# Attention with exponentials over blocks of three half steps, and the loop over batches written out

## The reference

```python
q = (xin @ wq.T + bq).reshape(b, s, H, DK)
k = (xin @ wk.T + bk).reshape(b, s, H, DK)
v = (xin @ wv.T + bv).reshape(b, s, H, DK)
scores = jnp.einsum('bshd,bthd->bhst', q, k) * (1.0 / np.sqrt(DK))
a = jax.nn.softmax(scores, axis=-1)
o = jnp.einsum('bhst,bthd->bshd', a, v).reshape(b, s, DH)
...
x1 = layernorm(xh + mha(xh, ...), g1, be1)
x2 = layernorm(xsh + mha(xsh, ...), g2, be2)    # xsh: the smoothed input
y = jnp.concatenate([x1, x2], axis=-1)
y_ff = relu(y @ w_ff1.T + b_ff1) @ w_ff2.T + b_ff2
out = x + layernorm(y + y_ff) + ffn(xn)
```

## Time and profile before

| what | us |
|---|---|
| median of 3 runs | 2676.5 (2676.16 to 2676.57) |
| the profiled execution | 2678.51 |
| its span, first to last instruction | 2677.0 |
| attention of one batch, first exponential to last | 492 to 498 |
| ACT, exponentials of attention, all | 1915.7 busy |
| PE, values (L1183) | 1071.4 busy |
| PE, scores (L1157) | 624.5 busy |

### The profile page before, as it was taken

How to read it: one execution, slowest core, us unless ns; L and a number is a source line. 1 busy time by engine, 2 the same in 40 slices (tenths; PEclk the granted TensorE clock), 3 DMA queues, 4 the chain that set the end, 5 groups by cost and what they waited for, 6 DMA issues and landing times.

```text
span 2677.0 us, 75084 instructions
## 1 busy us (share of the span) xinstructions
PE 2529.1 (94%) x30049; PEld 1004.4 (38%) x30049; DVE 1516.9 (57%) x3228; ACT 2190.8 (82%) x2411; POOL 355.2 (13%) x349
## 2 busy tenths in 40 slices
PE   5799999999999999998999999999999999999976
PEld 3233333335633333333663333333464333333344
DVE  5344555565764555556575455555567545555576
ACT  3699999994479999997449999999556999999933
POOL 0201010003410100000440101000144010100142
PEclk9899999999999999999999999999999999999988
DMA  4602010003120202000411102000041010100001
GB/s 159 122 10 34 10 34 10 10 10 104 50 65 10 34 14 38 10 6 12 115 49 57 30 14 34 10 10 6 21 122 48 10 34 10 34 10 10 6 25 45
DMA packets 50612, 96.38 MB, mean 36 GB/s; under 512 B 8768, under 2 KB 33344, under 8 KB 49872
## 3 DMA queue, kind: packets, MB, share of 16 engines
q1 hardware_dynamic: 41808, 71.99, 8.9%
q0 software_dynamic: 8448, 19.41, 4.4%
HBM read 57.23 MB, written 34.08 MB: 34 GB/s over the span
## 4 chain that ended last, share of the span: by engine, by line
PE 80%; DVE 7%; issue 5%; POOL 4%; ACT 1%; DMA 1%; SPq 0%; DVEq 0%; POOLq 0%; ACTq 0%
PE slot L1183 34%; PE slot L1157 20%; PE slot L994 16%; POOL p_sb L495 3%; PE slot L1227 2%; PE slot L1079 2%; PE slot L1215 2%; PE slot L1109 1%; DVE o_sb L679 1%; PE slot L1118 1%; PE slot L1107 1%; DVE hid_one L722 1%; DMA k_st<-part_dram 1%; PE slot L1060 1%; ACT p_sb L585 1%
## 5 line engine op out<-in xcount | busy, mean ns | idle before, releaser
L585 ACT ACTIVATE p_sb<-slot 128x1024 f32<-128x1024 f32 x2048 | 1915.7, 1029 | 125.1 <-PE slot L1157 122.4
L1183 PE MATMUL slot<-p_sb,v_sb 128*17 128x512 f32 x8192 | 1071.4, 597 | 23.2 <-DVE o_sb L679 12.6
L1157 PE MATMUL slot<-q_st,k_st 50*128 50x512 f16 x4096 | 624.5, 384 | 23.4 <-DMA k_st<-part_dram 15.4
L1157 PEld LDWEIGHTS slot<-q_st,k_st 50*128 50x128 f16 x4096 | 126.8, 94 | 896.4 <-ACT p_sb L585 715.8
L722 DVE TENSOR_SCALAR hid_one<-slot,b_grown 128x256 f32<-128x256 f32 x256 | 123.8, 484 | 298.9 <-PE slot L994 289.0
L1183 PEld LDWEIGHTS slot<-p_sb,v_sb 128*17 128x17 f32 x8192 | 180.2, 97 | 241.4 <-ACT p_sb L585 211.5
L734 DVE SCALAR_TENSOR_TENSOR second<-slot,second 128x256 f32<-128x256 f32 x64 | 27.2, 425 | 371.1 <-PE slot L994 371.1
L688 DVE RECIPROCAL rden<-den 128x256 f32<-128x256 f32 x128 | 224.4, 1753 | 7.5
L994 PE MATMUL slot<-xt_parts,w_parts 128*32 128x256 f16 x6144 | 214.8, 274 | 1.6 <-DVE hid_one L722 1.6
L994 PE MATMUL slot<-w_parts,hid_parts 128*32 128x256 f16 x6144 | 214.7, 274 | 0.0
L1227 PE MATMUL slot<-wf_parts,p_sb 128*128 128x256 f16 x1536 | 178.0, 275 | 8.7 <-POOL p_sb L495 8.6
(11 more groups left out here) (101 smaller groups left out, 1833.0 us busy)
## 6 DMA issues: line engine op xcount, KB each, us to landing
part_dram<-p_sb SPq DMA_DIRECT2D x16, 1024.0 KB, 4.0
q_st<-part_dram POOLq DMA_DIRECT2D x96, 128.0 KB, 7.9
xn<-x SPq DMA_DIRECT2D x16, 512.0 KB, 7.6
second<-x SPq DMA_DIRECT2D x32, 256.0 KB, 3.9
ffn_dram<-second SPq DMA_DIRECT2D x32, 256.0 KB, 2.0
area<-ffn_dram SPq DMA_DIRECT2D x16, 512.0 KB, 4.8
out<-area SPq DMA_DIRECT2D x16, 512.0 KB, 3.2
k_st<-part_dram SPq DMA_DIRECT2D x48, 128.0 KB, 12.3
```

The source lines that it names most:

```text
L585: act.activation(p_sb[:, n % 4, :], slot[n % 3][:, :], ACT.Exp, scale=0.25 / GROW ** 2).then_inc(exp_done, 1)
L1157: mm = pe.matmul(slot[at % 3][:, k * CHUNK:(k + 1) * CHUNK], k_st[rows_, pair, kt * P:(kt + 1) * P], q_st[rows_, pair, c_ * CHUNK:(c_ + 1) ...
L1183: mm = pe.matmul(o_bank[ROW * j:ROW * j + DK + 1, :], v_sb[:, a, kt, GH * g + j, :], p_sb[:, n % 4, (j % 2) * CHUNK:(j % 2 + 1) * CHUNK], ...
```

## The change

Scores, exponentials and values of attention are cut another way. A half step is now half of the queries of a tile: four heads by 256 queries, with four products of 256 columns where there were two of 512; pairs still run on the two row halves, and alternate banks. Half steps are grouped in blocks of three (slots 0, 1 and 2); a unit of 32 half steps has ten blocks of three and one of two. ACT takes slots 0 and 1 of a block in one exponential of 2048 columns and slot 2 in a second of 1024; the last block has only the first. The results go to two pairs of buffers: `p_first`, the four old buffers as two of 2048 columns, and `p_third`, two parts of `area`, which is free in attention.

PE's order: scores of block i, values of block i - 1, then a piece of the network or the projection. The scores' first two half steps wait for the first exponential of the block before, the third for its second; the values wait for the same two. For the first block of a unit all of them wait for the last exponential of the unit before. Values have twice as many products of half the columns. Network pieces are placed by blocks: 0, 1, 3, 4, 6, 8, 9, 10 (3 to 10 in unit 0), the projection by block 5. PSUM's four slots become one tensor.

The loop over batches is written out on every engine. A test buffer of the last batch (`weights_fine`) moves to another part of `area` and waits for the stores of the batch before.

```diff
+BLOCKS = [(3 * i, min(3 * i + 3, STEPS)) for i in range(-(-STEPS // 3))]
+LAST_BLOCK = len(BLOCKS) - 1
+EXPS = 2 * LAST_BLOCK + 1
+HALF_CHUNK = CHUNK // 2
...
-NET_KTS, FIRST_NET_KTS, PROJECTION_KT = [0, 2, 4, 6, 10, 12, 14, 15], [6, 8, 10, 11, 12, 13, 14, 15], 8
+NET_BLOCKS, FIRST_NET_BLOCKS, PROJECTION_BLOCK = [0, 1, 3, 4, 6, 8, 9, 10], [3, 4, 5, 6, 7, 8, 9, 10], 5
...
-        slot = [ctx.enter_context(nc.psum_tensor(f"slot{i}", [P, SLOT], f32)) for i in range(4)]
+        banks = ctx.enter_context(nc.psum_tensor("banks", [P, 4 * SLOT], f32))
+        slot = [banks[:, i * SLOT:(i + 1) * SLOT] for i in range(4)]
...
+        def batches_in_line(eng, prologue, middle, last):
+            prologue(0)
+            for b in range(B - 1):
                 middle(b)
             last(B - 1)
...
+            p_flat = p_sb[:, :, :].rearrange("p i n -> p (i n)")
+            p_first = p_flat[:, 0:2 * SLOT], p_flat[:, 2 * SLOT:4 * SLOT]
+            p_third = area[:, 3 * SLOT:4 * SLOT], area[:, 0:SLOT]
...
-                    hold(sp, pv_done, TILES * UNITS2 * (b + 1) + 2)
+                    hold(sp, pv_done, STEPS * UNITS2 * (b + 1))
...
-                    for n in range(UNITS2 * STEPS):
-                        act.wait_ge(scores_made, UNITS2 * STEPS * b + n + 1)
-                        if n % 2 == 0:
-                            act.wait_ge(pv_done, UNITS2 * TILES * b + n // 2 + 1)
-                        act.activation(p_sb[:, n % 4, :], slot[n % 3][:, :], ACT.Exp, scale=0.25 / GROW ** 2).then_inc(exp_done, 1)
+                    for unit in range(UNITS2):
+                        u = UNITS2 * b + unit
+                        for i, (lo, hi) in enumerate(BLOCKS):
+                            block = len(BLOCKS) * unit + i
+                            act.wait_ge(scores_made, EXPS * u + 2 * i + 1)
+                            if block >= 2:
+                                done = BLOCKS[i - 2][1] + (0 if i >= 2 else -STEPS)
+                                act.wait_ge(pv_done, STEPS * u + done)
+                            act.activation(p_first[block % 2], banks[:, 0:2 * SLOT], ACT.Exp, scale=0.25 / GROW ** 2).then_inc(exp_done, 1)
+                            if hi - lo == 3:
+                                act.wait_ge(scores_made, EXPS * u + 2 * i + 2)
+                                act.activation(p_third[block % 2], slot[2][:, :], ACT.Exp, scale=0.25 / GROW ** 2).then_inc(exp_done, 1)
...
-                        if a == 1 or not isinstance(b, int):
+                        if 2 * b + a > 0:
...
-                    flat = area[:, 0:2 * FF]
+                    dve.wait_ge(stored, 16 * (CHUNKS * (B - 1) + 1))
+                    flat = area[:, SLOT:SLOT + 2 * FF]
...
-                with step.over(B - 1, PER_MIDDLE) as b:
+                for b in range(B - 1):
...
-                    def scores(unit, kt):
+                    def scores(unit, i):
                         a, g, c_ = UNIT_LIST[unit]
-                        if kt == 0 and c_ == 0:
+                        u = UNITS2 * b + unit
+                        if i == 0 and c_ == 0:
                             hold(pe, stack_in[g], 16 * ((K_LOADS + 2 * Q_LOADS) * b + (Q_LOADS, K_LOADS + 2 * Q_LOADS)[a]))
                             if a == 0:
                                 hold(pe, k_first_in[g], 16 * K_LOADS * (b + 1))
-                        for n in (2 * kt, 2 * kt + 1):
-                            at = STEPS * unit + n
-                            pe.wait_ge(exp_done, UNITS2 * STEPS * b + at - 2 + 3)
-                            if at == 2:
-                                pe.wait_ge(ff_read, CHUNKS * b + 1)
-                            for k in range(2):
-                                pair, rows_ = GH // 2 * g + n % 2, slice(HALF * k, HALF * k + ROWS)
-                                mm = pe.matmul(slot[at % 3][:, k * CHUNK:(k + 1) * CHUNK], k_st[rows_, pair, kt * P:(kt + 1) * P],
-                                               q_st[rows_, pair, c_ * CHUNK:(c_ + 1) * CHUNK], start=True, stop=True)
-                            mm.then_inc(scores_made, 1)
-                    scores(0, 0)
-                    for unit, (a, g, c_) in enumerate(UNIT_LIST):
+                        lo, hi = BLOCKS[i]
+                        for n in range(lo, hi):
+                            if n == lo and (u > 0 or i > 0):
+                                pe.wait_ge(exp_done, EXPS * u + 2 * i - (1 if i else 0))
+                            if n == lo + 2:
+                                if u > 0 or i > 0:
+                                    pe.wait_ge(exp_done, EXPS * u + 2 * i - (0 if i else 1))
+                                if unit == 0 and i == 0:
+                                    pe.wait_ge(ff_read, CHUNKS * b + 1)
+                            kt, tok = n // 2, c_ * CHUNK + n % 2 * HALF_CHUNK
+                            for j in range(GH):
+                                pair, rows_ = GH // 2 * g + j // 2, slice(HALF * (j % 2), HALF * (j % 2) + ROWS)
+                                at = SLOT * (n - lo) + CHUNK * (j % 2) + HALF_CHUNK * (j // 2)
+                                mm = pe.matmul(banks[:, at:at + HALF_CHUNK], k_st[rows_, pair, kt * P:(kt + 1) * P],
+                                               q_st[rows_, pair, tok:tok + HALF_CHUNK], start=True, stop=True)
+                            if n >= lo + 1:
+                                mm.then_inc(scores_made, 1)
+                    def values(unit, i):
+                        a, g, c_ = UNIT_LIST[unit]
                         u = UNITS2 * b + unit
-                        net_kts = FIRST_NET_KTS if unit == 0 else NET_KTS
-                        for kt in range(TILES):
-                            if kt + 1 < TILES:
-                                scores(unit, kt + 1)
-                            elif unit + 1 < UNITS2:
-                                scores(unit + 1, 0)
-                            if kt in net_kts:
-                                (second_out_part if unit % 2 else second_hidden)(b, unit // 2, net_kts.index(kt))
-                            if kt == PROJECTION_KT and unit > 0:
+                        lo, hi = BLOCKS[i]
+                        block = len(BLOCKS) * unit + i
+                        if i == 0:
+                            pe.wait_ge(o_read, u + 1)
+                            if unit == 0:
+                                pe.wait_ge(ff_read, CHUNKS * b + 2)
+                        for n in range(lo, hi):
+                            if n == lo:
+                                pe.wait_ge(exp_done, EXPS * u + 2 * i + 1)
+                            if n == lo + 2:
+                                pe.wait_ge(exp_done, EXPS * u + 2 * i + 2)
+                            kt, cols = n // 2, slice(n % 2 * HALF_CHUNK, (n % 2 + 1) * HALF_CHUNK)
+                            p = (p_first if n < lo + 2 else p_third)[block % 2]
+                            for j in range(GH):
+                                at = SLOT * ((n - lo) % 2) + CHUNK * (j % 2) + HALF_CHUNK * (j // 2)
+                                mm = pe.matmul(o_bank[ROW * j:ROW * j + DK + 1, cols], v_sb[:, a, kt, GH * g + j, :], p[:, at:at + HALF_CHUNK],
+                                               start=(n == 0), stop=(n >= STEPS - 2), skip_group_check=True)
+                            mm.then_inc(pv_done, 1)
+                    for unit in range(UNITS2):
+                        net_blocks = FIRST_NET_BLOCKS if unit == 0 else NET_BLOCKS
+                        for i in range(len(BLOCKS)):
+                            scores(unit, i)
+                            if i > 0:
+                                values(unit, i - 1)
+                            elif unit > 0:
+                                values(unit - 1, LAST_BLOCK)
+                            if i in net_blocks:
+                                (second_out_part if unit % 2 else second_hidden)(b, unit // 2, net_blocks.index(i))
+                            if i == PROJECTION_BLOCK and unit > 0:
                                 out_projection(b, unit - 1)
-                            if kt == 0:
-                                pe.wait_ge(o_read, u + 1)
-                                if unit == 0:
-                                    pe.wait_ge(ff_read, CHUNKS * b + 2)
-                            pe.wait_ge(exp_done, STEPS * u + 2 * kt + 2 + 3)
-                            for j in range(GH):
-                                n = 2 * kt + j // 2
-                                mm = pe.matmul(o_bank[ROW * j:ROW * j + DK + 1, :], v_sb[:, a, kt, GH * g + j, :],
-                                               p_sb[:, n % 4, (j % 2) * CHUNK:(j % 2 + 1) * CHUNK],
-                                               start=(kt == 0), stop=(kt == TILES - 1), skip_group_check=True)
-                            mm.then_inc(pv_done, 1)
+                    values(UNITS2 - 1, LAST_BLOCK)
```

(10 more changed lines are left out.)

7 lines of the change are left out of this document (4 added, 3 removed).

## The result

The median after is 2756.6 us against 2676.5 before: a ratio of 1.030, 95% interval 1.028 to 1.032, so slower by 80 us. The forecast was 2763.

A forecast was written before the change was run, and what follows sets the result against it. PE was taken to set the attention unit at 30.7 us, ACT 1.3 us behind. Units 1 to 15 +76.5, unit 0 +15.3, first exponentials +0.9 and loop turns -6.4 made +86.3 us: 2763 us, range 2715 to 2825.

The forecast's parts named there:

- Units 1 to 15: Attention units after each batch's first: 32.3 us a unit against 30.7, +76.5 us over four batches.
- unit 0: First attention unit of a batch: PE stalls 5.2 us for DVE's copy, 37.0 us in batches 1 to 3; +15.3 us.
- all else: The span outside attention's unit windows: two loop turns saved, a later first exponential per batch; -5.5 us.
- The step on which all hung: PE's attention queue: third scores wait for the 1024-column exponential, ready values stand behind; blocks with pieces take 3.22 or 2.82 us.
- The margin of 0.2 a unit: Added to an attention unit's 32.1 us for the unnamed rest of what PE's sum missed before; 32.3 us.
- The loop: Loop over batches written out: PE's 3.1 us wait at each of two turns goes, -6.4 us.
- ACT's idle time: Sign in attention: ACT's idle time before exponentials grows from 125 us to some 250, released by PE's scores.
- Gain by sums: Rival: values or their loads pass the waiting third scores, a unit costs 29.4 us, kernel 2583 us; chance 0.11.
- Loads not hidden: Rival on score pairs: weight loads make a pair 0.132 us, kernel 2823 (chance 0.10); harder, 0.213 us, 3053 (chance 0.03).
- Clock: Rival: PE's idling in units drops its clock to half for 5 us a unit, +150 us, 2913 us; chance 0.04.
- Cover: Rival: waits covered better than thought, a unit 31.0 us, unit 0 unhurt, 2676 us or little more; chance 0.03.

## Why the prediction was right

By the spans the change was +78.3 for +86.3. Units 1 to 15 came out 8.6 us under their term, unit 0 3.9 over and all else 3.3 under, of which 2.5 are the early first exponential of this one execution. So the total owes a little to errors that offset each other, but its main term stands on spacings that were measured.

**The step on which all hung** held: the third scores wait for T in PE's queue, values that are ready stand behind them, and F keeps two of three slots. Eleven spacings came out within 0.04 of the forecast, and freeing the queue (values ahead of the third scores) took 0.22 to 0.25 off exactly the blocks named. F at 1.88 with the next at 1.77, pairs of scores at 0.109 apart, values at 0.43 a half step and 0.10 a change of shape were all as taken from the nearest rows.

**The margin of 0.2 a unit** was wrong: units are 32.11. It stood for what the sum of the old kernel left over, 0.5 a unit, and came to 12 us over 60 units. The run with the pieces moved shows 0.22 of the 0.5 to be the o_sb wait (0.44 in every second unit), which goes in the new order. The other 0.28 is in all old units (30.48 for my 30.2). I take it for short waits of PE on single exponentials, which that sum of streams left out and the new one, worked out wait by wait, had in it; that wasn't measured by itself. What is measured is that the new sum needed no margin. The stops in block 4, which I didn't foresee, put 3 us back, and the term was 76.5 for 67.9.

**Unit 0** was undersized: 39.2, 38.9 and 37.9 for 37.0, while batch 0 didn't grow (32.7 for 33.8). The stall itself was right: DVE's copy ended 17.5 us after the first exponential for my 17.9. The term that failed is PE's clock, which I had only as a rival for later units. After the stall PE ran at the lower level. In the last batch this cost about 0.7 us up to the start of block 5 (20.0 us after the first exponential; without the margin my sum gives 19.3) and 0.4 in block 5 (3.47 for 3.08). In batches 1 and 2 block 5 took 4.74 and 4.39: there the clock was still at the lower level (mean of 0.60 over batch 1's block 5, 777.93 to 782.67, against 0.82 over the last batch's, 2118.54 to 2122.01), and that is nearly all by which these two exceed the last batch. They also had the lower level in block 1, where a window shows

```profile
761.00:765.00 4.00, 4.00 (x44) 0.57 0.00 0
```

(PE busy 4.00 of 4.00 us, clock 0.57, no DMA), and the block took 4.1 us for 2.68. But those 1.4 us don't count: the stall ends by DVE's time, and took them up (block 4 is 7.4 there for 8.7, and block 5 starts 20.0 to 20.1 us after the first exponential in all three). PE's waits ahead of block 1 are the same in the last batch, 1.76 and 0.30, and its clock didn't fall there; what decides that stays open. In the kernel before the clock fell in unit 0 too (0.91 to 0.92 in the loop), but by less.

**The loop** brought more than its two turns. The turns gave 9.8 us for 6.4, then took some 7.6 back in unit 0, which I had not joined to them: the stall was worked out from the last batch, where no turn helps. The lower unit of the written-out batch was in the prices, and rightly so: written out, where waits are compared with constants, a unit is shorter in the old order (15 take 461 for 465.9) and in the new (32.11 for 32.47).

**ACT's idle time** before exponentials is 232 us for some 250.

**The rivals.** Gain by sums: no unit came near 29.4 (the least is 30.46, with a third of the pieces' work), and the order changed so as to allow it came to 32.05. Loads not hidden: twelve score products, six pairs with two loads of 128 columns each, are recorded at 0.83 us, as six quads of network products are the earlier trace rows; so these loads cost nothing here. The Trainium skill, "TensorE: Matmul & The Clock Gate", section LDWEIGHTS (loading the stationary operand), gives columns / 1.2, 107 ns for 128, by which I estimate two such loads a pair at 0.21 us. The trace after disagrees with 0.109, as the rows before did. Clock: not inside units 1 to 15 (1.00 in all four windows), though PE waits there in several blocks of each unit; only in unit 0. Cover: no.

**What stays open.** After the last exponential the changed kernel takes 137.0 us, as do the old order with the loop written out (136.9) and that with the pieces moved (137.1), against 133.9 before and 133.8 with the blocks in the loop. So it belongs to the loop written out, 3 us, and the traces place it behind all work: DVE's last operation ends 127.4 us after the last exponential with the loop and without, and the rest of the span is 6.4 us with the loop and 9.2 to 9.8 without, in all nine kernels that have it written out. There GpSimd's closing instruction (a DRAIN of 4.87 us) starts 4.1 to 4.7 us after DVE's last operation; with the loop it starts 1.3 after it. What makes GpSimd late wasn't tried. Nor was what stops PE on issue, or what in the order by blocks, apart from the width of F, costs 11 us a batch.

## What to carry to other kernels

Where an in-order engine feeds another through few buffers, don't add up busy times: follow who holds which slot until when, and what stands behind the wait. A wider instruction saves its fixed cost (0.05 us each here) but can't start before the last of its inputs is there (0.2 us in each block of 3.22 here, none in those of 2.84); with three slots that was a loss of 36 us. Price a written-out loop and a new order apart, and look for what a wait you remove had covered. And before such a rebuild, try where the fillers stand: moving two pieces of a unit by one tile gained 11 us here (spans of 2655.5 and 2644.3).

## What the runs showed of the hardware

- DVE's operation on 128x4 at L655 took 6.80 us beside one GpSimd operation of 9.95 (the rows of unit 0 above), and 6.78 and 6.77 at the same place in batches 2 and 1; the median of the 48 operations of that line is 0.17, as of others of this kind:

```profile
2647.35 0.17 DVE L662 TENSOR_TENSOR rs<-rs 128x8 f32<-128x8 f32 x1
```

- PE stops for 0.2 to 2.4 us in the middle of a group of like products, with nothing shown that holds it, in units in which POOL issues refills: 31 times in the seven kernels with blocks, never in the four with the old order. Instructions themselves are fetched by DMA, in more packets in the changed kernel than the 251 before. All 31 stops end 2.5 to 3.6 us after such a packet starts (3.1 to 3.2 in the five of the changed kernel), however long they are; the stop shown above began 0.1 us after one. Most packets bring no stop (72 in units 1 to 15 of batch 1, with one stop). That points to late fetches, but no run tested it.

```profile
q8 instruction: 334, 5.47, 0.8%
```

- In the loop, where waits are compared with a register, a block that PE sets takes about 0.08 us more (3.30 for 3.22 in a block); between the recorded end of scores and the exponential behind them the timelines show 0.12 in the loop and 0.04 written out.
- A change between products on row halves and on column quarters costs 0.10 us, in every kernel here.
